# Start-up of a two-layer language-model tower on one core: w_proj's sums earlier, chunk 2's statistics and step 2's squares in a new order, eight unread matmuls, chunk 1 transposed a gate later

## What is computed

```
h   = take(embed_table, ids)                      # ids [64,256], table [32768,256]
x   = layernorm(h)
f, i = sigmoid(x Wf^T), sigmoid(x Wi^T)           # 256 wide
g   = x Wh^T ; cand = g + 0.5 where g >= 0, else sigmoid(g)
s_t = f_t * s_(t-1) + i_t * cand_t                # along the 256 tokens, s_0 = 0.5
h   = h + s
x   = layernorm(h)
r   = relu(x W_fc^T + gate * (x v^T fast_b^T u^T))  # 1024 wide, W_fc ternary times a row scale
out = h + (r*r) W_proj^T                          # W_proj ternary times a row scale
```

## Time and profile before

| | |
|---|---|
| median of 3 runs | 915.22 us (912.91 to 915.28) |
| profiled execution | 913.92 us, its span 912.10 us |
| PE busy | 880.3 us, 97% of the span |
| ACT busy | 788.5 us, 86% |
| DVE busy | 755.8 us, 83% |
| POOL busy | 418.5 us, 46% |
| mean granted TensorE clock | 0.998 of full speed |
| step 1, 2, 3: first gate matmul starts at | 35.65, 66.89, 97.75 us |

### The profile page before, as it was taken

How to read it: one execution, slowest core, us unless ns; L and a number is a source line. 1 busy time by engine, 2 the same in 40 slices (tenths; PEclk the granted TensorE clock), 3 DMA queues, 4 the chain that set the end, 5 groups by cost and what they waited for, 6 DMA issues and landing times.

```text
span 912.1 us, 18335 instructions
## 1 busy us (share of the span) xinstructions
PE 880.3 (97%) x5505; PEld 482.1 (53%) x5505; DVE 755.8 (83%) x1338; ACT 788.5 (86%) x1195; POOL 418.5 (46%) x457
## 2 busy tenths in 40 slices
PE   4979999999999999999999999999999999999997
PEld 2435554555555455555455555545555545555554
DVE  6988888788888888888888888888888888888766
ACT  5677998888998888998888899888889988899884
POOL 7446544445544445554444554444555444433110
PEclk9999999999999999999999999999999999999999
DMA  4123434432333443333443233344333334423311
GB/s 146 24 53 68 92 73 87 99 78 69 89 82 75 98 98 61 79 85 74 91 98 78 68 88 82 75 97 98 63 81 89 73 85 97 97 51 82 78 47 47
DMA packets 225372, 72.88 MB, mean 80 GB/s; under 512 B 200134, under 2 KB 220176, under 8 KB 225344
## 3 DMA queue, kind: packets, MB, share of 16 engines
q1 hardware_dynamic: 219200, 68.33, 33.8%
q0 software_dynamic: 6144, 4.21, 2.0%
HBM read 27.68 MB, written 24.64 MB: 57 GB/s over the span
## 4 chain that ended last, share of the span: by engine, by line
PE 85%; DVE 4%; ACT 4%; issue 2%; DMA 2%; SPq 1%; POOL 1%; ACTq 0%; POOLq 0%; DVEq 0%
PE bank L848 33%; PE bank L870 22%; PE y_ps L784 22%; PE bank L884 3%; PE turned L824 1%; ACT sq L584 1%; PE turned L761 1%; ACT normed L509 1%; ACT relu L571 1%; SPq L338 1%; DMA x_cols<-x_rows 1%; PE turned L772 1%; PE turned L771 1%; DMA spill<-hid_blocks 1%; DVE hid L1277 0%
## 5 line engine op out<-in xcount | busy, mean ns | idle before, releaser
L870 PE MATMUL bank<-x_cols,fc_t 128*128 128x512 f16 x1024 | 244.1, 381 | 3.6 <-ACT relu L571 3.6
L420 POOL TENSOR_SCALAR var_eps<-moments 128x4 f32<-128x4 f32 x64 | 59.5, 929 | 387.9 <-DVE moments L1020 387.6
L848 PE MATMUL bank<-x_cols,w_hi 128*128 128x512 f16 x768 | 229.8, 381 | 4.9 <-ACT forget L560 2.0
L848 PE MATMUL bank<-x_cols,w_lo 128*128 128x512 f16 x768 | 229.4, 380 | 0.0
L784 PE MATMUL y_ps<-proj_t,sq_hi 128*128 128x256 bf16 x1024 | 225.6, 273 | 3.0 <-DVE sq_lo L1203 3.0
L784 PE MATMUL y_ps<-proj_t,sq_lo 128*128 128x256 bf16 x1024 | 225.6, 273 | 0.0
L571 ACT ACTIVATE relu<-bank,relu_scale 128x512 f32<-128x512 f32 x256 | 159.3, 689 | 39.6 <-PE bank L884 39.0
L410 POOL DMA_INDIRECT rows_raw<-table,idx_now x128 | 148.0, 1156 | 59.9 <-issue 30.8
L870 PEld LDWEIGHTS bank<-x_cols,fc_t 128*128 128x128 bf16 x1024 | 95.0, 98 | 130.8 <-issue 28.3
L1203 DVE TENSOR_TENSOR sq_lo<-sq,sq_hi 128x1024 f16<-128x1024 f32 x128 | 150.6, 1214 | 5.8 <-ACT sq L584 5.7
L509 ACT ACTIVATE normed<-h,shift,rstd 128x256 f32<-128x256 f32 x256 | 132.7, 601 | 5.4 <-POOL shift L428 5.4
(11 more groups left out here) (143 smaller groups left out, 919.7 us busy)
## 6 DMA issues: line engine op xcount, KB each, us to landing
out<-out_sb SPq DMA_DIRECT2D x31, 512.0 KB, 3.0
spill<-hid_blocks SPq DMA_DIRECT2D x30, 256.0 KB, 2.1
hid_rows<-spill SPq DMA_DIRECT2D x120, 64.0 KB
rows_raw<-table,idx_now POOLq DMA_INDIRECT x128, 2.6
x_cols<-x_rows SPq DMA_TRANSPOSE x120, 3.6
sq<-w_fc SPq DMA_DIRECT2D x1, 1024.0 KB, 5.5
pj_raw<-w_proj SPq DMA_DIRECT2D x1, 1024.0 KB, 4.8
out<-out_sb SPq DMA_DIRECT2D x2, 256.0 KB, 2.1
```

Of the source, the lines that this page charges most:

```text
L848: ins = pe.matmul(gate_bank(p, par)[:, :], w[:, k, q, :], x_part(0, par, part)[:, :, k, :], start=(k == 0 and w is w_hi and part == 0), st ...
L870: ins = pe.matmul(fc_bank(f, par)[:, :], fc_t[:, f, k, :], x_part(1, 0, part)[:, :, k, :], start=(opens and k == 0 and part == 0), stop=(n ...
```

## The change

Seven edits, all in the start-up (before step 3).

1. PE: `keep_busy(8)`, eight matmuls of 512 columns whose result nobody reads, ahead of the first `turn_normed(0)`; they wait for the scaled weights w_hi. `turn_low_rank` moves from behind gate 0 to ahead of it; on DVE `scale_low_rank` moves ahead of `cols_low(0)`.
2. PE: `turn_normed(0, 1)` (chunk 1) moves from behind gate 3 to behind gate 4 of step 0.
3. ACT: the two sums over |w_proj| move from the end of step 0 to behind the first evict. DVE: the scales made of them move ahead of the first recurrence of step 1, the ternary weights behind `residual(1, 1)`.
4. DVE: `measure(0, 1)` moves ahead of `split_low_rank`; chunk 2's `guard`, `guard_sum` and `measure` move from the end of step 0 and the start of step 1 to directly behind `residual(0, 0)`, ahead of `split_u` and `set_relu_scale`; `cols_low(1)` is now ahead of `set_relu_scale`.
5. ACT, step 1: `normalise(0, 2)` ahead of `low_high(0)`; the squares 1, 2 and 3 of the eight-block move partly into step 2.
6. ACT, DVE and PE, step 2: half 0 of the gates is taken in the order forget, inp, cand_sig, cand_lin, with squares in between; `part_high(1)` stands behind `normalise(0, 3)` and ahead of `x_high(0, 3)`; on DVE `measure(0, 3)` stands behind `x_low(1, 1)`.
7. PE, end of step 1: `spread_proj_scale` ahead of `turn_hidden(1)`.

The diff, cut:

```diff
@@ ScalarE, step 0
                 if start:
                     evict(0, par, 0, 0, forget, ACT.Sigmoid)
+                    act.wait_ge(pj_in, 16)
+                    for k in range(KD):
+                        act.activation(pj_a[:, k, :], pj_raw[:, k, :], ACT.Abs, accum_out=pj_s[:, 0, k:k + 1])\
+                            .then_inc(abs_summed, 1)
                     evict(0, par, 0, 1, inp, ACT.Sigmoid)
...
@@ ScalarE, steps 1 and 2
                     part_high(0)
+                    normalise(0, 2, h0[:, 0, :, :])
                     low_high(0)
-                    normalise(0, 2, h0[:, 0, :, :])
                     x_high(0, 2)
-                    back(1)
+                    for f in range(4):
+                        clip(0, f, par)
+                    square_high(0, 0)
+                    clip(0, 4, par)
+                    clip(0, 5, par)
+                    square(0, 0)
+                    clip(0, 6, par)
+                    clip(0, 7, par)
                     return
                 if second:
-                    evict_low()
+                    square_high(0, 1)
+                    evict(2, par, 0, 0, forget, ACT.Sigmoid)
+                    square(0, 1)
...
+                    square_high(0, 3)
+                    square(0, 3)
                     normalise(0, 3, h0[:, 1, :, :])
+                    part_high(1)
                     x_high(0, 3)
-                    part_high(1)
@@ TensorE
+            def keep_busy(times):
+
+                pe.wait_ge(w_hi_ready, 3)
+                for _ in range(times):
+                    pe.matmul(bank[3][:, :], w_hi[:, 0, 0, :], w_hi[:, 0, 0:4, :], start=True, stop=True)
+
+            keep_busy(8)
             turn_normed(0)
+            turn_low_rank()
...
-                    gate(0)
-                    if start:
-                        turn_low_rank()
-                    gate(1)
-                    gate(2)
+                    for p in range(3):
+                        gate(p)
...
                     gate(3)
+                    gate(4)
                     if start:
                         turn_normed(0, 1)
-                    gate(4)
@@ VectorE, start
+            scale_low_rank()
             cols_low(0)
-            scale_low_rank()
             guard(1, 64, 1)
             guard_sum(1, 1)
-            split_low_rank()
             dve.wait_ge(h0_ready, 2)
             measure(0, 1, h0[:, 1, :, :])
+            split_low_rank()
@@ VectorE, step 0, behind residual(0, 0)
-                    split_u()
-                    set_relu_scale()
                     guard(2, 64, 0)
                     guard_sum(2, 0)
+                    dve.wait_ge(h0_ready, 3)
+                    measure(0, 2, h0[:, 0, :, :])
+                    split_u()
                     return
@@ VectorE, step 2
+                if second:
+                    square_low(0, 0)
+                    square_low(0, 1)
+                    square_low(0, 2)
+                    x_low(1, 1)
+                    measure_next()
+                    square_low(0, 3)
+                    candidate(0)
+                    weigh(0)
+                    scan(0)
+                    turn_blocks()
+                    x_low(0, 3)
+                    scale_output(0)
+                    part_low()
...
```

More of the change, by code:

```diff
@@ L631, in step @@
                     scale_fc(0)
-                    act.wait_ge(pj_in, 16)
-                    for k in range(KD):
-                        act.activation(pj_a[:, k, :], pj_raw[:, k, :], ACT.Abs, accum_out=pj_s[:, 0, k:k + 1])\
-                            .then_inc(abs_summed, 1)
                     return
@@ L842, in gate @@
                     else:
-                        pe.wait_ge(gate_taken, 8 * n + ((1, 2) if start else (4, 3))[p - 4])
+                        pe.wait_ge(gate_taken, 8 * n + ((1, 2) if start or second else (4, 3))[p - 4])
                     q = 2 * g + e
@@ L857, in free @@
                     elif front:
-                        pe.wait_ge(gate_taken, 8 * n + (2, 5, 6, 8)[f])
+                        pe.wait_ge(gate_taken, 8 * n + (4 if second else 2, 5, 6, 8)[f])
                     else:
@@ L943, in step @@
                 wide(6, False)
-                if first:
-                    turn_hidden(1)
                 wide(7, False)
@@ L948, in step @@
                     spread_proj_scale()
+                    turn_hidden(1)
             steps(pe, step)
@@ L1251, in candidate @@
                 def candidate(e):
-                    dve.wait_ge(gate_taken, 8 * n + (8 if e else 4 if start else 2))
+                    dve.wait_ge(gate_taken, 8 * n + (8 if e else 4 if start or second else 2))
                     dve.tensor_tensor(cand[:, e, :], cand_lin[:, e, :], cand_sig[:, e, :], ALU.max)\
@@ L1260, in weigh @@
                     if e == 0:
-                        dve.wait_ge(gate_taken, 8 * n + (2 if start else 3))
+                        dve.wait_ge(gate_taken, 8 * n + (2 if start or second else 3))
                     wait(dve, scanned, 4 * (n - 1) + 2 * e + 2)
@@ L1269, in scan @@
                     if e == 0:
-                        dve.wait_ge(gate_taken, 8 * n + (1 if start else 4))
+                        dve.wait_ge(gate_taken, 8 * n + (1 if start or second else 4))
                     if e == 0 and steady:
@@ L1345, in step @@
                     mark_below(pj_raw, pj_a, pj_s, range(KD))
+                    residual(1, 1)
                     make_ternary(pj_raw, pj_a, pj_s, pj_c, range(KD), pj_ready)
                     set_proj_scale()
-                    residual(1, 1)
-                    guard(3, 64 * 2, 1)
                     guard_sum(3, 1)
+                    return
+                if second:
[12 more added lines that the diff above has]
+                    part_low()
+                    low_low()
+                    candidate(1)
+                    weigh(1)
+                    scan(1)
+                    emit(0, 0, 0)
+                    guard(4, 64 * 2, 0)
+                    residual(2, 0)
+                    guard_sum(4, 0)
                     return
@@ L1367, in step @@
                     turn_blocks()
-                if second:
-                    x_low(0, 3)
                 scale_output(n - 2)
                 part_low()
-                if ahead and not second:
+                if ahead:
                     x_low(0, n + 1)
```

14 lines of the change are left out of this document (10 added, 4 removed).

## The result

The changed kernel takes 921.05 us (median of 4 runs, 920.64 to 921.58) against 915.22 before: ratio 1.0071, 95% interval 1.0055 to 1.0087. Five more timed runs, beside 15 of before on one chip, gave 1.0080 (1.0067 to 1.0093). It is slower by some 6 us (5.8 between the two medians, 6.5 by the ratio, which is not their quotient), outside the forecast range of 913.0 to 919.6; slower had 0.28 of the chances.

The account below looks back on a forecast made before the run. TensorE bounds the kernel from step 3 on, so start-up changes carry to the end: +0.86 (low_sums late) +1.8 (clock) -0.62 (DMA wait) = +2.0 us, 915.95 profiled, 917.2 on the median; range 913.0 to 919.6.

Parts of the forecast that it names:

- normalise(1, 1) at S2 + 7.85: Step 2, ScalarE: gates, squares and evicts let normalise(1, 1) start 7.85 us after step 2's first gate matmul.
- Start: 1.0 us won: Start-up: statistics moved ahead bring step 1's first gate matmul (S1) from 35.65 to 34.6 us.
- keep_busy is 0: Start of step 0, TensorE: the eight unread matmuls neither win nor cost time, 0 us.
- root(1, 0) over 3.2 us long: Step 1, GpSimd: a sign that VectorE's moved guard passes delay root(1, 0), making it last over 3.2 us.
- S2 = 64.95: Step 2's first gate matmul (S2) comes at 64.95 us instead of 66.89, 1.95 won.
- S2 later than 66: Sign of being wrong: step 2's first gate matmul comes later than 66 us.
- low_sums, behind part_lo, 24.5 after S2: Step 2, TensorE: low_sums waits for part_lo until 24.5 us after step 2's first gate matmul, 89.45, 0.86 late.
- A gap of 5 us opens in PE: Step 2, TensorE ahead of low_sums: a wait of 5 us where 0.56 was.
- The clock falls in it, +1.8: Step 2, TensorE: its clock falls in the 5 us gap ahead of low_sums, costing 1.8 us, bounds 0 and 3.4.
- S3's DMA wait goes: Step 3's first gate matmul (S3) no longer waits 0.62 us for the DMA.
- The slower side: Step 2, low_sums to step 3: clock stays low and root(0, 3) takes its upper value, +4.2, 919.4 us; chance 0.15.
- The two with fewer falls of the clock: Steps 1 and 2, TensorE: one clock fall less, 915.5 us, chance 0.30; no fall, -1.5, 913.7 us, chance 0.13.

Follow-up runs that it names:

- e5: The changed kernel with one more GpSimd wait, so the clearing of chunk 3's rows starts only once VectorE has set the bound: 919.48 us, ratio 1.0056.
- e1: The changed kernel with step 2's orders and ScalarE's squares at the end of step 1 as before: 915.12 us, ratio 1.0014.
- e4: The changed kernel with six more unread matmuls in the wait before step 1's first gate: 919.16 us, ratio 1.0066.
- e7: The changed kernel with the last w_proj sums and their scale ahead of residual(1, 1) again: 919.38 us, ratio 1.0068.
- after_again: The changed kernel run and profiled a second time, no edit: 920.45 us, ratio 1.0080.
- e11: The changed kernel with the first three low parts of squares of chunk 0 made plain copies instead of differences: 919.71 us, ratio 1.0064.
- e6: The kernel before with only the start of the change (unread matmuls, low-rank and chunk 1 turns, ScalarE's w_proj sums, measure(0, 1)): 916.52 us, ratio 1.0030.
- e8: The changed kernel with step 2's orders and step 1's last squares as before, and chunk 3's clearing waiting for the bound: 913.78 us, ratio 0.9993.
- e9: The changed kernel with chunk 3's clearing waiting for the bound, and guard_sum and statistics (0, 3) directly behind residual(1, 1): 914.36 us, ratio 1.0003.
- e2: The changed kernel with statistics (0, 3) ahead of the first three low parts of squares in step 2: 916.0 us, ratio 1.0020.

## Why the prediction was wrong, point by point

The step that failed is the chain to part_lo in step 2, and in it the term "normalise(1, 1) at S2 + 7.85": it priced ACT's queue and put root(1, 1) on GpSimd at nothing. The row is at S2 + 10.67, because the shift of that root was held for 3.70 us. That is 2.8 of the 3.4 us by which low_sums comes later behind S2 than forecast. The other 2.8 us are those by which S2 is late. Before's own trace had a row that speaks against 7.85: there the same shift ends at 75.97, 9.08 behind S2, in a root that ran beside two sq_lo.

```profile
75.76 0.21 POOL L428 TENSOR_TENSOR shift<-minus_mean,rstd 128x4 f32<-128x4 f32 x1
```

- **Start: 1.0 us won. Wrong by 0.9.** The chain did start 1.2 earlier (statistics at 24.30, against 25.52 in the earlier trace rows) and GpSimd's shift came 1.3 earlier. What failed is "the same chain, moved": the small scale steps of DVE between them moved too, into the clearing that follows the gathers, and stalled 1.6 us. With that gone (e5) S1 is 34.31, forecast 34.6.
- **keep_busy is 0. Right about S1; that it is free isn't borne out.** Gate 0 had the high clock (20.12, pairs 0.43 apart), and S1 didn't move by it. It isn't always so: in three of the twelve profiles with the eight matmuls (e1, e4, e7) gate 0 ran mostly at the low clock even so, 0.57 to 0.61 in 20 to 24 us. That a longer wait before S1 would let the clock fall behind it was not in the sum: 1.27 us where it happens. And without them it is 0.16 to 0.22% less in two pairs that are barely told apart, for a reason that stays open.
- **root(1, 0) over 3.2 us long: right.** 46.74 to 49.98, 3.24 against 2.49. cols_low(1) waits for ACT now (52.60), as said.
- **S2 = 64.95. Wrong by 2.8**: 0.9 from S1, 1.3 from the low clock behind it, the rest in step 1. The second low stretch came as forecast, and lasted longer (0.50 in 53 to 58). The prediction's own sign of being wrong, S2 later than 66, was met, and in after_again (66.80) too.
- **low_sums, behind part_lo, 24.5 after S2. Wrong: 27.86**, and this is the step that decides. Its first term, normalise(1, 1) at S2 + 7.85, took ACT's queue as the limit. The row is S2 + 10.67 (78.42): root(1, 1) was never priced. I had read in the earlier trace rows that a DVE pass holds a small GpSimd instruction, used it on root(1, 0) and root(0, 3), and passed over the one root whose DVE neighbours changed most. I also took each GpSimd instruction to lose one pass; the shift lost the rest of one and three in a row. The remaining 0.5 us are root(0, 3), 3.88 us up to ACT's start where 3.45 was in the sum (3.45 to 4.05 stated). The Trainium skill, "SBUF — State Buffer", section "SBUF: two separate sides", calls the shared port pair an exclusive lock held for a whole instruction. The trace agrees for var_eps and minus_mean, which each ended 0.09 behind the pass beside them. The shift goes beyond it: it waited through passes back to back to the end of the last (78.33), 3.70 us. Why the shift and not the others is open. The same section counts casts and tensor_scalar among what can take the pair; e11's casts, which held the shift, and u_pow, a TENSOR_SCALAR held beside the clearing, agree.
- **A gap of 5 us opens in PE. It did, in two parts**, 2.94 at 86.46 for sq_lo and 3.46 at 95.61 for part_lo, since the fourth low part of squares also stands behind x_low(1, 1). The first is a wait I hadn't in the chain at all.
- **The clock falls in it, +1.8. Right in some executions, and nearer 1.3.** In this profile it fell in the first part (0.59 in 86 to 90) and not behind the second (1.00 from 96 on), in after_again behind both. Of the nine profiles that wait 2.9 to 5.1 us at low_sums, it fell behind that wait in six, with 9.53 to 9.87 us from low_sums to S3 against 8.37: 1.2 to 1.5 us for one fall.
- **S3's DMA wait goes: right.**
- **The rivals.** The slower side came nearest in size (+4.2, measured +6.2 at S3), by another mechanism: not 3.4 us of low clock between low_sums and S3 (none there in this profile), but a later part_lo. The two with fewer falls of the clock left the size of the chain to part_lo untouched, which is what was off.
- **Sum.** Forecast +2.0 at S3, measured +6.23: S2 2.8 later than forecast, part_lo 3.4 later, clock behind low_sums 1.8 less, and -0.2 elsewhere. In after_again the same total (+6.6) is made up otherwise: S2 1.85 late, and a fall of the clock behind low_sums.

From the experiments, with some 0.1% on each figure and partly between chips, the loss of 0.80% splits so: start alone +0.30 (e6); with the rest but step 2's orders +0.14 (e1), so step 0's end and step 1 gave back 0.16; step 2's orders +0.66.

## What to carry to other kernels

When a change moves a large pass of VectorE, list every small GpSimd instruction that will now run beside it, and put statistics there, not copies, differences or sums: the position of one `measure` was worth 5 us here. Then ask what stands behind the held chain in each queue. A shift held for 2.56 us cost next to nothing where the statistics (0, 3) stood ahead of x_low(1, 1) (e1); held for 3.70 us with the statistics behind that x_low, it helped to make root(0, 3) 6.5 us late, counted from step 2's first gate. And when a chain is moved earlier, its unmoved neighbours (a clearing, a gather) now meet other instructions. Last, profile the changed kernel twice before a fall of the clock is given a price: here two profiles of one kernel had it at different places.

## What the runs showed of the hardware

- A GpSimd shift of 128x4 numbers that had started beside a two-input DVE pass waited through three more in a row (3.70 or 3.71 us in eight profiles), through two more (2.56 in e1 and e8), through three casts (2.10), and not at all beside BATCH_NORM_STATS2 (0.20 in e9).
- That is no rule for every small instruction. In the 16 profiles var_eps stood 910 times beside such a pass with the next one right behind it, and minus_mean 450 times. They took 0.90 to 1.18 us and got through behind the first pass each time, as in the earlier trace rows.
- The other way round, a GpSimd memset of 128x1024 held a DVE instruction of 128x8 for 1.76 us, from 30.68 to its own end near 32.4, though the memset's row starts only at 31.43. With a wait ahead of the memset its row starts at 31.51 and the same DVE instruction takes 0.17 (e5). A two-input pass of 128x512 beside that memset was not held: 0.69 from 31.64 in e5, and from 32.97 before.
- After the same wait of 2.81 us before step 1 the granted clock was 1.00 in one execution of the changed kernel and 0.57 in another. Over all profiles it fell behind that wait in five of seven; where the wait was 1.46 to 2.59 us, in none of eight. The runs of one kernel, e2, differ by up to 3.9 us.
- The clock's record does not show the first low stretch: in 20 to 24 us of before it says 1.00, while the pairs of matmuls start 0.83 apart (0.43 at the high clock). There the spacing is what tells.
